# Relative attention's value products: query chunks on the column tiles, relative values in the same bank

## What is computed

```python
rk, rv = embK[idx], embV[idx]          # idx = clip(key - query, -64, 64) + 64
logits = jnp.einsum('bhqd,bhkd->bhqk', q, k) + jnp.einsum('bhqd,qkd->bhqk', q, rk)
w = jax.nn.softmax(logits, axis=-1)
out = jnp.einsum('bhqk,bhkd->bhqd', w, v) + jnp.einsum('bhqk,qkd->bhqd', w, rv)
```

## Time and profile before

| what | value |
|---|---|
| median of 3 runs | 4265.67 us (4260.19 to 4268.16) |
| span of the profiled execution | 4272.5 us |
| own time of the profiled execution | not given beside its span |
| TensorE matmul busy | 3916.3 us (92%) |
| VectorE busy | 3446.8 us (81%) |
| ScalarE busy | 2970.6 us (70%) |
| GpSimd busy | 1500.0 us (35%) |
| relative attention, first to last gather | 228.0 to about 1972 us |

### The profile page before, as it was taken

The page is one execution under the profiler, slowest core; times in us unless marked ns, Lnnn a source line. Parts: engine busy times, 40 slices in busy tenths (PEclk is TensorE's granted clock), DMA queues, the critical chain, the costliest instruction groups (busy, mean ns, idle before and its releaser), DMA issues. The chain is left out here.

```text
span 4272.5 us, 78522 instructions
## 1 busy us (share of the span) xinstructions
PE 3916.3 (92%) x26838; PEld 2067.2 (48%) x26838; DVE 3446.8 (81%) x6397; ACT 2970.6 (70%) x5963; POOL 1500.0 (35%) x1461
## 2 busy tenths in 40 slices
PE   8699999999999999996879999999999999759998
PEld 5344545545455445543533333333333333659998
DVE  7788888888888888862778889898888884657776
ACT  4077878778878777884218888888888887236666
POOL 0356666666666665652110000001010100533333
PEclk9599999999999999998969999999999999779999
DMA  8666666667677767643773333334243331679997
GB/s 315 156 162 162 163 165 168 161 163 168 163 165 168 166 161 169 167 120 108 243 155 60 64 60 64 61 56 77 47 72 56 63 53 41 160 264 325 322 326 222
DMA packets 479567, 636.81 MB, mean 149 GB/s; under 512 B 61752, under 2 KB 404520, under 8 KB 464960
## 3 DMA queue, kind: packets, MB, share of 16 engines
q1 hardware_dynamic: 460640, 608.46, 55.7%
q0 software_dynamic: 18528, 23.34, 2.9%
HBM read 413.78 MB, written 216.78 MB: 148 GB/s over the span
## 5 line engine op out<-in xcount | busy, mean ns | idle before, releaser
L399 DVE TENSOR_REDUCE pa_pm<-pa_psA 128x2 f32<-128x1024 f32 x1024 | 1208.3, 1219 | 133.5 <-PE pa_psA L484 133.3
L1122 ACT ACTIVATE ra_p<-ra_psS 128x512 f32<-128x512 f32 x2048 | 1082.4, 605 | 316.1 <-PE ra_psS L1199 224.2
L1033 DVE TENSOR_REDUCE ra_pm<-ra_psA 128x1 f32<-128x896 f32 x1024 | 1113.2, 1087 | 157.1 <-PE ra_psA L1157 142.2
L458 ACT ACTIVATE pa_p<-pa_psS 128x512 f32<-128x512 f32 x2048 | 1063.4, 603 | 245.9 <-PE pa_psS L510 241.7
L510 PE MATMUL pa_psS<-pa_qs,pa_zs 50*128 50x512 f32 x2048 | 792.1, 464 | 77.9 <-ACT pa_p L458 63.9
L484 PE MATMUL pa_psA<-pa_zs,pa_qs 48*128 48x512 f32 x2048 | 795.6, 471 | 38.4 <-DMA pa_zs<-k_halves 18.2
L1157 PE MATMUL ra_psA<-ra_zs,ra_qs 48*128 48x512 f32 x2048 | 730.7, 451 | 19.3 <-DVE ra_pm L1035 8.4
L1199 PE MATMUL ra_psS<-ra_qs,ra_zs 50*128 50x512 f32 (+3 forms) x2176 | 699.7, 407 | 28.9 <-ACT ra_p L1122 20.7
L510 PEld LDWEIGHTS pa_psS<-pa_qs,pa_zs 50*128 50x128 f32 x2048 | 341.6, 184 | 625.4 <-ACT pa_p L458 609.2
L1230 PE MATMUL ra_psO<-ra_p,ra_vs 128*32 128x512 f32 (+3 forms) x6400 | 552.8, 450 | 0.0
L1199 PEld LDWEIGHTS ra_psS<-ra_qs,ra_zs 50*128 50x128 f32 x2176 | 351.1, 186 | 412.1 <-ACT ra_p L1122 318.1
(11 more groups left out here) (247 smaller groups left out, 4995.7 us busy)
## 6 DMA issues: line engine op xcount, KB each, us to landing
mo_w_parts<-second_weight_parts SPq DMA_DIRECT2D x39, 2048.0 KB
relative_rows<-ra_rst SPq DMA_DIRECT2D x128, 512.0 KB
ra_blk<-window_rows SPq DMA_DIRECT2D x128, 512.0 KB, 4.6
ra_zs<-k_halves SPq DMA_DIRECT2D x192, 248.0 KB, 7.6
mo_w_raw<-ffn_W SPq DMA_DIRECT2D x39, 1024.0 KB, 11.6
ra_dl<-relative_rows SPq DMA_DIRECT2D x128, 256.0 KB, 5.5
window_rows<-ra_pc SPq DMA_DIRECT2D x128, 256.0 KB, 4.4
pa_qs<-q_halves SPq DMA_DIRECT2D x192, 128.0 KB, 6.4
```

The lines of the kernel that those rows point to most:

```text
L399: dve.reduce_max(pm[:, par, 2 * a:2 * a + 2], psA[w][:, :, :], AX.X).then_inc(s_am.h, 1)
L458: act.activation(pr[:, i % NPR, :], psS[:, slot(i), :], ACT.Exp).then_inc(s_ex.h, 1)
L1033: dve.reduce_max(pm[:, q, i, 2 * left:2 * left + 1], psA[w][:, lo:lo + 2 * G - P], AX.X).then_inc(s_far.h, 1)
L1122: act.activation(dst, psS[:, slot(i), :], ACT.Exp if kind == "E" else ACT.Copy).then_inc(s_cp.h, 1)
```

## The change

In each step the four column tiles now hold one tile of each of the four query chunks. The window tiles of the chunks come in steps 3 and 4, 7 and 8, 11 and 12, 14 and 15 (`W_STEP`); every other place is an E tile. `psO` gathers all 16 steps of a head, with chunk c in partitions 32c to 32c+31. The relative values are multiplied into the same bank at the end of step 15, which also closes the sum. ScalarE copies `psO` once a head into `ra_ob` (now two buffers). The products with `sel`, the tile `ra_ot`, three of the four evacuations, VectorE's copy and the gather's turn of `psA` are gone. A head has 37 turns, so the bank of a turn now depends on the head too. The steps of the collection of sums begin one group later.

```diff
+W_STEP = (3, 7, 11, 14)
+def ring_steps():
+    far, out = [0] * 4, []
+    for k in range(STEPS):
+        step = []
+        for c in range(4):
+            if k in (W_STEP[c], W_STEP[c] + 1):
+                step.append(("W", c, k - W_STEP[c]))
+            else:
+                step.append(("E", c, far[c]))
+                far[c] += 1
+        second = any(kind == "W" and j for kind, _, j in step)
+        step.sort(key=lambda x: (x[0] == "W") != second)
+        out.append(step)
+RING = [x for step in RING_STEPS for x in step]
+for _at, _c in ((38, 0), (54, 1), (66, 3), (67, 2)):
     RING.insert(_at, ("F", _c, 0))
...
-RTURNS = TURNS + len(R_STEPS)
+RTURNS = TURNS - 1 + len(R_STEPS)
...
                 if kind == "F":
-                    s_fm.wait(act, t + 1)
+                    s_us.wait(act, STEPS * t)
...
-            def evacuate(t, c):
-                s_us.wait(act, STEPS * t + 4 * c + 4)
-                s_fm.wait(act, t + 1)
-                act.activation(ot[:, c * G:(c + 1) * G], psO[:, :], ACT.Copy).then_inc(s_oev.h, 1)
+            def keep_head(t):
+                s_us.wait(act, STEPS * (t + 1))
+                s_ob.wait(act, 64 * (t // UN - 1))
+                act.activation(ob[:, t // UN % 2, t % UN, :], psO[:, :], ACT.Copy).then_inc(s_nf.h, 1)
...
-            def gather_heads(t, w):
-                s_oev.wait(pe, 4 * t)
-                s_cp.wait(pe, NR * (t - 1) + place["F", 3, 0] + 1)
-                for c in range(4):
-                    pe.matmul(psA[w][32 * c:32 * c + 32, 0:G], sel[:, :], ot[:, c * G:(c + 1) * G],
-                              start=True, stop=False, tile_position=(0, 32 * c), skip_group_check=True)
-                for c in range(4):
-                    last = pe.matmul(psA[w][32 * c:32 * c + 32, 0:G], evc[:, :], ptr[:, c * G:(c + 1) * G],
-                                     start=False, stop=True, tile_position=(0, 32 * c), skip_group_check=True)
-                last.then_inc(s_fm.h, 1)
...
             def weigh(t, p, k):
                 s_cp.wait(pe, NR * t + bank_at[4 * k + 3] + 1)
                 if k == 0:
                     s_v.wait(pe, 4 * (t + 1))
+                    s_nf.wait(pe, t)
-                if n == 0:
-                    s_oev.wait(pe, 4 * t + c)
...
+                for n, (kind, c, j) in enumerate(RING_STEPS[k]):
+                    bank = (4 * k + n) % NPR
+                    if kind == "E":
+                        todo.append([(z, c, bank, lo, hi) for z, lo, hi in pieces(c, j)])
+                    else:
+                        z0 = (0 if j else NROT) + 4 * c
+                        todo.append([(z0 + i, c, bank, i * P, (i + 1) * P) for i in range(4)])
                 for turn in range(4):
                     for tile in todo:
                         if turn < len(tile):
+                            z, c, bank, lo, hi = tile[turn]
+                            last = pe.matmul(psO[32 * c:32 * c + 32, lo:hi], v[:, z, :], pr[:, bank, lo:hi],
+                                             start=k == 0, stop=False, tile_position=(0, 32 * c),
+                                             skip_group_check=True)
+                if k == STEPS - 1:
+                    s_cp.wait(pe, NR * (t + 1))
+                    for c in range(4):
+                        last = pe.matmul(psO[32 * c:32 * c + 32, :], evc[:, :], ptr[:, c * G:(c + 1) * G],
+                                         start=False, stop=True, tile_position=(0, 32 * c), skip_group_check=True)
                 last.then_inc(s_us.h, 1)
```

More of the change, by code:

```diff
@@ L573 @@
 W = 2 * P
[L574 to L577, removed]
+W_STEP = (3, 7, 11, 14)
[12 more added lines that the diff above has]
+        out.append(step)
+    assert far == [14] * 4
+    return out
+RING_STEPS = ring_steps()
+RING = [x for step in RING_STEPS for x in step]
+for _at, _c in ((38, 0), (54, 1), (66, 3), (67, 2)):
     RING.insert(_at, ("F", _c, 0))
@@ L586 @@
 REL_ORDER = "saasOsaas"
-RC_REL = 30
-SUM_TURNS = (13, 18, 23, 28)
+RC_REL = 29
+SUM_TURNS = (12, 17, 22, 27)
 def rel_turns():
@@ L611, in rel_turns, with rel_attention @@
     return out
-def rel_attention(nc, ident, sel, masks, qd, kd, vd, e_stack, evc, ev_side, dr_r, dr_p, den_d, rec_d, ot_rows):
+def rel_attention(nc, ident, masks, qd, kd, vd, e_stack, evc, ev_side, dr_r, dr_p, den_d, rec_d, ot_rows):
     body = rel_turns()
@@ L906, in _ @@
             s_mq.wait(sp, 16 * NP2 * HEADS)
[L907 to L910, removed]
+            gather_denominators(HEADS, HEADS // UN - 1)
+            spread_reciprocals(HEADS // UN - 1)
+            store_o(HEADS, HEADS // UN - 1)
+            s_ob.wait(sp, 64 * (HEADS // UN))
         @blk.gpsimd
@@ L1091, in _ @@
                             keep_r(t + 2, a, w)
-                        elif kind == "M":
+                        else:
                             split_m(t + 1, w)
[L1094 to L1097, removed]
                         if n in SUM_TURNS:
                             sum_right(t, SUM_TURNS.index(n))
-                        if p % 2 == 0 and n == RC_REL:
-                            invert(2 * it + p // 2)
-            keep_head(HEADS, 0, PT % 2)
-            invert(HEADS // UN)
-            s_ir.wait(dve, 64 * (HEADS // UN + 1))
-            dve.tensor_tensor(out=ob[:, :, :], in0=ob[:, :, :], in1=recb[:, :, :], op=ALU.mult).then_inc(s_ml.h, 1)
+                        if p % 2 == 0 and t >= UN and n == RC_REL:
+                            invert(t // UN - 1)
+            last = HEADS // UN - 1
+            invert(last)
+            s_ir.wait(dve, 64 * (last + 1))
+            dve.tensor_tensor(out=ob[:, last % 2, :, :], in0=ob[:, last % 2, :, :], in1=recb[:, :, :], op=ALU.mult
+                              ).then_inc(s_ml.h, 1)
         @blk.scalar
@@ L2562, in program @@
             rel_projection(nc, A, ident, sel, masks, e_stack, evc, ev_side, q2, kl2, kr2, v_rows)
-            rel_attention(nc, ident, sel, masks, q2, k_sides, v_rows, e_stack, evc, ev_side, dr_r, dr_p,
+            rel_attention(nc, ident, masks, q2, k_sides, v_rows, e_stack, evc, ev_side, dr_r, dr_p,
                           den_d[0:UN, :], rec_d[0:UN, :], ot_rows)
```

70 lines of the change are left out of this document (26 added, 44 removed).

## The result

The changed kernel takes 4299.85 us (median of 13 runs, 4269.11 to 4307.5), the kernel before on the same chips 4268.26 us (13 runs, 4260.19 to 4278.5). The ratio is 1.0068, with a 95% interval of 1.0054 to 1.0082: **slower by 0.7%**, where 4233 us were forecast, range 4192 to 4258. Sign and range are wrong.

The account below looks back on a forecast made before the run. VectorE was taken to set the pace for about five steps after the gather, TensorE for the rest. Terms summed to -0.93 us a head over 31 heads, -1.5 last head, -1.8 at the end: -32, giving 4233 us, range 4192 to 4258.

Parts of the forecast that it names:

- Step 6: GpSimd and SyncE: later scaling and DMAs hidden by idle time, wait for folded windows can grow; 0, at most 0.3 us.
- step 1: The gather leaves step 2 of each head; VectorE, next behind TensorE, limits the saving: -1.30 us a head.
- step 3: ScalarE loses three of four evacuations a head, which counts only through TensorE's waits for its copies: -0.4 us a head.
- Step 4: The two W tiles of a chunk stand together in three chunks instead of one, saving TensorE time: -0.2 us a head.
- Step 2: Four products with `evc` come to the end of step 15, where nothing hides them: +0.97 us a head.
- Step 5: In `weigh`, a W tile's short products beside three long ones in eight steps cost nothing: 0 us a head.
- Short pieces queue: Rival: in the eight W steps, short products end after the long ones, 6.0 us a head, 4425 us; chance 0.10.
- Nothing left over: Rival: VectorE paces the whole head, added `evc` work and GpSimd's wait cancel the saving, 4257 us; chance 0.13.
- The evacuations were the pace: Rival: ScalarE's evacuations from three-bank `psS` held up the head, which shortens by 2.2 us, 4194 us; chance 0.20.

Follow-up runs that it names:

- the new order: SyncE's queue reordered so that window-weight stores go ahead of relative-product stores: ratio 0.9942 in the changed kernel (0.991 in an earlier batch), 0.9985 in the kernel before.
- first and third profile: The changed kernel with nothing further altered, profiled in its first measurement (4299.85 us) and its third (4296.7 us, ratio 1.0074).
- second profile: The changed kernel with nothing further altered, measured and profiled again: 4309.99 us, ratio 1.0065.
- the last order: The changed kernel with SyncE's first stores alternating between window weights and relative products, window weights first: 4227.81 us, ratio 0.9917.

## Why the prediction was wrong

**Step 6 failed.** It named the right wait ("TensorE's wait for the folded windows ... can grow") and then placed its chain "between ScalarE's exp of step 7 and the fill of step 11 ... where little is saved; I take 0, and 0.3 as the other end". The chain begins at VectorE's copy in step 2, one line of the earlier trace rows that I read for its length only, and passes through SyncE's queue, for which no row was read. So the saving of 1.3 us of step 1 lay inside the chain. Two signs that the prediction itself named as wrong came: a longer wait for the folded windows, and heads of over 54.2 us. What the runs showed in its place: the wait grows from 13.6 to 28.6, 35.2 and 35.5 us in 28 heads, 0.5 to 0.8 us a head, and behind the longer waits the clock falls, for which the sum had no term. Taking the chain away gives the changed kernel 1.2 to 1.5% and the old one 0.15%. Without it the change stands at 0.9957 or below in place of 1.0065 to 1.0074, so the chain, with the falls that it brings, accounts for the wrong sign. No run measures waiting and clock apart; the heads of the profiles give an estimate. Over 28 heads of the stage, those that no fall touches have a mean of 54.8 us before and 54.9, 55.3 and 55.2 after, which makes 3 to 13 us; what the touched ones are longer than that comes to 8 us in all before and 20, 29 and 25 after, 12 to 22 us more (the long wait ahead of the fall is in it). So by this estimate more than half of the loss lies in heads with a fall of the clock, for which the sum had no term at all.

**Steps 1, 3 and 4** (-1.30, -0.4 and -0.2, together -1.9) can be told only together. With the chain away the head goes from 54.32 to 53.92, -0.40. Take out +0.75 for the `evc` group, and -1.15 is left for the three. (This is a difference of two kernels' heads and of a run with falls of the clock, and no measurement.) The direction was right and the size too hopeful by some 0.75 us a head. The waits view says where most of it went: with the new order, TensorE's waits for VectorE in 300 to 1850 us are 0.8 us in the kernel before and 42 in the changed one, 1.4 us a head. Of these 0.85 us in nearly every head stand before the copy of the relative products, of the 1.85 us that step 1 saves there. Step 1 took VectorE to be next behind TensorE, and still let it take back too little. And the waits row that step 3 leaned on fell only from 15.1 to 13.2 us, 0.07 us a head.

**Step 2**, +0.97, measured +0.75 by the head: the group takes 0.96 us on TensorE, and about a fifth of it does not show in the head.

**Step 4** alone stays open. It compared W tiles side by side with two score products between them, and no run has that pair of arrangements. What was measured is side by side against far apart, +0.35 for side by side. Less waiting is not the reason: in 300 to 1850 us the named waits of TensorE are 50 us with the tiles side by side and 64 far apart, though the heads are shorter there.

**Step 5**, 0, was right: 0.99 us for a group with a W tile. *Short pieces queue*, the rival that gave the sign as it came out, is refuted by that row: the sign was right for another reason. By the rule of the Trainium skill, page "TensorE: Matmul & The Clock Gate", Part 3 (matmuls end in program order), that group should have taken about 1.75 us by the working of the prediction; the trace does not agree. *Nothing left over* had the wait for GpSimd in it, at 0.3 us, and is nearest in mechanism, but at 4257 us it had no way to come out slower. *The evacuations were the pace* (4194) is refuted: with every GpSimd wait gone the change is worth 18 us.

With the chain away the forecast of -32 us stands against about -18 where the two kernels ran beside each other: the savings were too hopeful, but the sign was right. What turned the sign was the chain beside the terms.

## What to carry to other kernels

Before you count a saving on the leading engine, look for waits on that engine that last longer than others and follow each back to its first cause, through the DMA queues: a store that is late only because the one ahead of it in the queue waits for another engine starts a chain that no busy share shows. If the saving lies beside such a chain, it turns into waiting, and work that is moved out of the chain's cover is paid for (here 0.75 of 0.97 us). Then try the order on the queue too: in the kernel before it was worth 0.15%, but in the changed one 1.2 to 1.5%, and it made a gain of the change.

## What was unexpected of the hardware

A single short wait in a stage where TensorE is otherwise 94 to 97% busy can be followed by a long fall of the clock. Behind 1.54 us of waiting it stood at 0.50 to 0.54 (the level of 1.2 GHz) from 532 to 553 us, behind 1.71 us at 0.57 over 22 us. In the stretch of 300 to 1850 us all falls of the changed kernel's first and third profile stand behind waits of 1.39 us or more, and the kernel whose waits are all 0.8 us or less has none; in the second profile one of six stands behind 1.33 us, for VectorE. This is no threshold. Of the waits in the third profile, seven of 1.37 to 1.61 us had no fall behind them. In the kernel with the W tiles far apart falls came behind 0.88 us, and in the kernel before with the new order one came behind 0.53 us, while the changed kernel with the last order had 28 waits of up to 0.9 us and none. In the kernel without the relative values some falls had no wait that I could name. The Trainium skill, page "TensorE: Matmul & The Clock Gate", Part 1, asks for loops without long idle gaps on TensorE; the trace agrees in direction, and shows that single waits as short as those above can have a fall behind them. Time and clock go together from execution to execution: the profiled executions of the changed kernel have spans of 4271.9, 4287.1 and 4319.9 us at mean clocks of 0.953, 0.951 and 0.944.
